# Filling the pair table with blank rows during the second layer instead of the first

## The reference, cut to what matters

```python
# x, ctx: 64 tiles of 128 tokens, 256 features, f32
x = x + ssm(layernorm(x))                    # layer 0: convolution, state space mix, gate
x = x + rope_attention(layernorm(x), ctx)    # 16 heads
x = x + recurrence(layernorm(x))             # scanned over the 64 tiles
x = x + gqa_attention(layernorm(x))          # layer 1: 16 heads on 4 kv heads
x = x + cross_attention(layernorm(x), ctx)   # one head of 256
# mixture of experts
scores = sigmoid(xf @ gate_w.T + lb_bias)
topw, topi = top_k(scores, 2)                # 8 experts, two for each token
for e in range(8):
    sel = (topi == e).any(-1)
    wmean = (topw * (topi == e)).sum() / max((topi == e).sum(), 1)
    out = out + where(sel, mlp_e(xf) * wmean, 0)
x = x + out + shared_mlp(xf)
```

## Time and profile before

| | us |
|---|---|
| median of 3 runs | 3413.04 |
| lowest and highest | 3412.17, 3423.11 |
| the profiled execution, its own time | 3413.31 |
| its span | 3411.5 |
| granted clock over the span | 0.969 of full speed |

### The profile page before, as it was taken

One profiled execution on the slowest core, in us unless ns is written; L12 is line 12 of the kernel. 1 busy time (PEld: TensorE's weight loads), 2 busy tenths in 40 slices (PEclk: granted clock), 3 DMA queues, 4 the chain that ended last, 5 costly groups with the idle time before them and its releaser, 6 DMA issues. The chain is left out here.

```text
span 3411.5 us, 95859 instructions
## 1 busy us (share of the span) xinstructions
PE 3081.2 (90%) x27055; PEld 2659.9 (78%) x27056; DVE 2776.1 (81%) x8725; ACT 2258.2 (66%) x8248; POOL 1512.2 (44%) x5113
## 2 busy tenths in 40 slices
PE   6589999999999999999998698999999999499998
PEld 4478888888888888888887577777777777387998
DVE  5588888888888888888885588888888887687776
ACT  3377777777777777777775477777777777143333
POOL 1244444545444444445452155555555554133333
PEclk8699999999999999999999799999999999699999
DMA  6111111111111111111110200000000000023443
GB/s 187 34 39 49 47 41 41 41 47 48 41 41 41 43 51 43 41 41 41 47 48 14 61 20 15 18 15 18 16 18 18 15 19 13 4 105 119 132 136 89
DMA packets 123391, 161.87 MB, mean 47 GB/s; under 512 B 27331, under 2 KB 94832, under 8 KB 123312
## 3 DMA queue, kind: packets, MB, share of 16 engines
q1 hardware_dynamic: 111056, 126.37, 12.7%
q0 software_dynamic: 12256, 34.53, 2.9%
HBM read 102.85 MB, written 61.53 MB: 48 GB/s over the span
## 5 line engine op out<-in xcount | busy, mean ns | idle before, releaser
L385 POOL TENSOR_TENSOR tiny<-tiny 128x1 f32<-128x1 f32 x3456 | 773.3, 224 | 800.0 <-DVE tiny L372 559.2
L802 ACT ACTIVATE work<-bank,att 128x128 f32<-128x128 f32 x2048 | 720.1, 377 | 55.9 <-DVE att L792 50.1
L802 ACT ACTIVATION_READ_ACCUMULATOR work<-bank,att 128x1 f32 x2048 | 444.5, 217 | 0.0
L792 DVE TENSOR_REDUCE att<-bank 128x4 f32<-128x512 f32 x512 | 333.8, 683 | 44.8 <-PE bank L785 44.8
L821 PE MATMUL bank<-const,work 128*128 128x128 f32 x2048 | 317.9, 278 | 30.6 <-ACT work L802 25.8
L785 PEld LDWEIGHTS bank<-work 32*128 32x128 f32 x4096 | 253.2, 189 | 105.7 <-issue 73.9
L1281 DVE SCALAR_TENSOR_TENSOR work<-work,small 128x127 f32<-128x127 f32 (+2 forms) x1152 | 317.7, 345 | 16.5 <-ACT work L1121 11.1
L785 PE MATMUL bank<-work 32*128 32x128 f32 x4096 | 301.9, 286 | 20.6 <-ACT work L1166 2.5
L821 PEld LDWEIGHTS bank<-const,work 128*128 128x128 f32 x2048 | 239.3, 142 | 73.5 <-ACT work L802 56.7
L385 POOL TENSOR_TENSOR tiny<-tiny,const 128x1 f32<-128x1 f32 x1152 | 251.6, 218 | 90.2
L185 PE MATMUL bank<-w1r,workr 128*128 (+2 forms) x802 | 267.8, 334 | 0.4 <-issue 0.2
(11 more groups left out here) (357 smaller groups left out, 8467.5 us busy)
## 6 DMA issues: line engine op xcount, KB each, us to landing
work<-decay_sums SPq DMA_DIRECT2D x64, 512.0 KB, 3.6
work<-pair_rows SPq DMA_DIRECT2D x91, 258.0 KB, 2.7
pair_rows<-extra SPq DMA_DIRECT2D x128, 182.0 KB
work<-in_ctx SPq DMA_DIRECT2D x128, 128.0 KB, 2.1
x_res<-in_x POOLq DMA_DIRECT2D x8, 1024.0 KB, 16.8
recurrence_out<-r_xo_ SPq DMA_DIRECT2D x64, 128.0 KB, 1.7
work<-recurrence_out SPq DMA_DIRECT2D x64, 128.0 KB
out_dram<-work POOLq DMA_INDIRECT x91, 2.8
```

The lines of the kernel that those rows point to most:

```text
L385: e.tensor_tensor(out_, a_, b_, ALU.add if b_ is three_halves else ALU.mult)\
L792: e.tensor_reduce(a_nm[:, 4 * g:4 * g + 4], sc_banks[g % 2][:, :].rearrange("p (h k) -> p h k", k=P), AX.X, ALU.max, negate=True).then_inc ...
L802: last = e.activation(Pb[g % 2][:, c * P:c * P + P], sc_banks[g % 2][:, c * P:c * P + P], ACT.Exp, bias=a_nm[:, 4 * g + c:4 * g + c + 1], ...
```

## The change

`blank_rows` and all that belongs to it moves from `layer0` to `layer1`. The 64 pieces, three DMAs each, keep their size. In layer 1 SP issues piece i-2 at the end of step i, behind `load_context(i-2)`. The sources are no longer buffers of their own: `blank` is `bo_row`, and `blank_end` is four columns of `tiny`. POOL can clear `bo_row` only when it has been read, so it waits for `b_vrow` first, and SP waits for `blank_ready` ahead of step 0 of layer 1, that is ahead of the first `load_output` and of all loads of the experts' weights. At the end of layer 1 SP waits until all blank rows have landed.

```diff
@@ layer0, sync
-                    b = i
-                    if live(b):
-                        blank_rows(b)
-
-                e.wait_ge(S["blank_ready"], 2)
+
                 pipeline(e, 4, step)
                 e.wait_ge(S["r_store"], 16 * NB)
-                e.wait_ge(S["blank"], 3 * 16 * NB)
@@ layer0, gpsimd
-                e.memset(blank_end, 0.0)
-                e.memset(blank, 0.0).then_inc(S["blank_ready"], 1)
-                e.wait_ge(S["blank_ready"], 1)
-                e.iota(blank_end[:, 2:3].bitcast(I32), [[0, 1]], base=TOKENS, channel_multiplier=1)\
-                    .then_inc(S["blank_ready"], 1)
@@ layer1
+        blank, blank_end = bo_row, tiny[:, 64:68]
@@ layer1, sync
+                def blank_rows(b):
...
+                    for at, n_, of in ((0, D, blank), (D, D, blank), (2 * D, 4, blank_end)):
+                        e.dma_start(rows_b[:, :, at:at + n_], of[0:n // 2].unsqueeze(1).to_broadcast([n // 2, 2, n_]))\
+                            .then_inc(S["blank"], 16)
@@ in step(i)
                     b = i - 2
                     if live(b):
                         load_context(b)
+                    b = i - 2
+                    if live(b):
+                        blank_rows(b)
...
+                e.wait_ge(S["blank_ready"], 2)
                 pipeline(e, 2, step, 0, expert_weights)
+                e.wait_ge(S["blank"], 3 * 16 * NB)
@@ layer1, gpsimd
+                e.memset(blank_end, 0.0)
+                e.wait_ge(S["b_vrow"], 1)
+                e.memset(blank, 0.0).then_inc(S["blank_ready"], 1)
+                e.wait_ge(S["blank_ready"], 1)
+                e.iota(blank_end[:, 2:3].bitcast(I32), [[0, 1]], base=TOKENS, channel_multiplier=1)\
+                    .then_inc(S["blank_ready"], 1)
```

More of the change, by code:

```diff
@@ L105 @@
         c_rec c_rinv c_rtr c_rT c_o c_ohi c_olo c_proj c_x2 r_stats r_aggr r_seed r_rs r_xn r_tr r_xnT r_fi
-        r_tfi r_go r_tg r_xo r_store r_a r_b r_d blank_ready blank
+        r_tfi r_go r_tg r_xo r_store r_a r_b r_d
     """.split(),
@@ L116 @@
         d_nmax d_exp d_ptr d_pt d_pv d_rinv d_x5 g_stats g_aggr g_seed g_rs g_xn g_tr g_xnT g_lg
-        g_sum
+        g_sum blank_ready blank
     """.split(),
@@ L749, in decoder @@
         slots = nc.dram_tensor("pair_rows", (SLOTS * P, ROW), F32, kind="Internal").ap()
-        blank, blank_end = wk(D), wk(4)
         def head_cols(blk, odd, g):
@@ L889, in store_output @@
                     e.dma_start(tile(xo_dram, b), r_xo_[:, :]).then_inc(S["r_store"], 16)
[L891 to L898, removed]
                 def step(i):
@@ L1591, in _ @@
                 e.dma_start(dbv_row, d_bv.partition_broadcast(P)).then_inc(S["l1_bias"], 16)
+                def blank_rows(b):
+                    n = SLOTS * P // NB
+                    rows_b = slots[0:NB * n].rearrange("(b p s) d -> b p s d", b=NB, p=n // 2)
+                    rows_b = rows_b[b] if isinstance(b, int) else rows_b[ds(b, 1)].rearrange("o p s d -> p (o s) d")
+                    for at, n_, of in ((0, D, blank), (D, D, blank), (2 * D, 4, blank_end)):
+                        e.dma_start(rows_b[:, :, at:at + n_], of[0:n // 2].unsqueeze(1).to_broadcast([n // 2, 2, n_]))\
+                            .then_inc(S["blank"], 16)
                 def load_output(b):
```

## The result

The changed kernel takes 3458.4 us (median; 3451.2 to 3473.5) where the kernel before takes 3415.6 in the same comparison: a ratio of 1.0129, 95% interval 1.0112 to 1.0146. It is slower by 43 us. Its profiled execution took 3454.8 us, with a span of 3453.0 against 3411.5, so the two traces differ by 41.4 us.

| part of the program | forecast | measured |
|---|---|---|
| up to SP's first issue of layer 1 (mostly layer 0's loop) | -12 | -5.3 |
| from there to the first L1880 (L1874 after) | +2.8 | +1.3 |
| from there to that line's last run, in layer 1's last step | +48 | +46.2 |
| the experts' part, behind it | 0 | -0.8 |
| sum | +38.8 | +41.4 |

A forecast was written before the change was run, and what follows sets the result against it. Neither loop was taken as bound by transfer bandwidth; time on SP's queue counted, with a ring through SP setting layer 1's step after the change. 3413.3 - 12 + 2.8 + 48 = 3452 us, range 3404 to 3483.

The forecast's parts named there:

- what bounds layer 1: Layer 1's loop: blank issues delay the recurrence's tile, so L1880 runs 0.8 us late in 60 steps, +48 us.
- ring: Layer 1: L1880 to PE's L1660, context's issue, blank issues, tile's landing, L1880 again; 16.13 us a step against 15.33.
- Layer 0's term: Layer 0's loop: decay sums issued some 2 us sooner, DVE's wait on them goes; -12 us, lower bound 5, upper 58.
- the floor at 0.73 us: Layer 0: PE/ACT and POOL chains hold the step, so of DVE's 0.96 us wait only 0.23 us a step returns.
- The start of layer 1: SP waits for POOL's cleared buffer ahead of the first tile and weight loads: +2.8 us, bounds 2.3 and 3.5.
- A: The forecast itself: the ring through SP sets layer 1's step, 3452 us, between 3425 and 3483; chance 0.70.
- D: Rival, layer 1: L1880 has more slack than read, issues are hidden, the loop costs nothing; 3404 us, chance 0.10.
- B: Rival, faster: the wait for the sums is layer 0's ring, all 58 us come back; 3394 us, chance 0.10.
- C: Rival, layer 1: open blank writes hold the tile's semaphore, landing 3.7 us, loop costs 150 us; 3554 us, chance 0.07.

The follow-up runs named there:

- the second experiment: Kernel before, with its blank writes kept in layer 0 but issued ahead of store_output instead of behind load_context: 3411.9 us, ratio 0.9995.

## Why the prediction was right

The step of **what bounds layer 1** held in each part. The forecast was a ring of 9.64 + 0.17 + 4.22 + 2.1 = 16.13 us; the terms measured 9.64, 0.17, 4.16 and 2.07 in the median, and the step 16.05. The loop's +46.2 us is made of 59 steps by 0.72 = 42.5, 1.7 in the first four steps, and some 2 in steps longer than the median (the loop is 6.6 us above 59 median steps, before it was 4.7). The last is no more than traces with the same median step differ by: the kernels at 15.33 have loops 1.9 to 4.7 us above 59 median steps. What decided the size was to take the context's issue to the next issue from layer 0, whose three instructions are the same, and to ask whether the lateness of L1880 comes back to the context's release. It does, and so it isn't paid once but in every step.

**Layer 0's term was mis-sized.** It was -12, from 54.6 - 57 x 0.73; it measured -5.3 between the two traces and 4.4 in the mean of all, at its own lower bound. The step that failed is taking the floor at 0.73 us, so that 0.23 us a step come back; 0.07 to 0.10 did. The reason was named there as the bound's: POOL's chain ends up to 0.1 us later when DVE runs beside it. It ended 0.09 later in the median, 0.12 in the steps shown. The floor was taken from a step in which DVE still waited, and what becomes the bound was priced at the speed that it had under the old schedule. The wait moved from L1307 to L1343, 54.6 to 49.3 us. Whether PE's and ACT's chain to the taps, which ends beside it, would have allowed more is open: no run made POOL's chain shorter with the rest left alone.

**The start of layer 1 was mis-sized too**, +1.3 where +2.8 stood with a lower bound of 2.3. SP's delay was as said: 3.14 us between the bias row and the first tile, 0.40 before. The step that failed is "PE had waited 2.66 us for the first of them, so there is no cover". A load issued later was used sooner. From issue to use the first tile took 3.67 us before (1885.74 to 1889.41) and 2.21 after, and the load of r_tfi_ that PE waits for 3.40 and 2.18. All traces agree: 3.15 to 3.67 us for the first tile where it goes out 0.4 us behind the bias row's load, 1.99 to 2.21 where SP was held first:

```profile
1883.16 0.34 SPq L1584 DMA_DIRECT2D work<-recurrence_out  x1
...
1884.02 0.43 SPq L1606 DMA_DIRECT2D r_tfi_<-in_L_ffn_expert_up_w  x1
```
```profile
1885.37 0.42 DVE L1874 TENSOR_TENSOR work<-work,rows 128x256 f32<-128x256 f32 x1 [2.81 <-DMA work<-recurrence_out]
```
```profile
1886.20 1.11 PE L1621 MATMUL bank<-const,r_tfi_ 128*128 128x128 f32 x4 [4.11 <-DMA r_tfi_<-in_L_ffn_expert_up_w]
```

Of the 2.74 us by which SP was held, 1.3 to 1.4 reached DVE and PE. Why the earlier loads took longer was not tried; the bias row's transfer, 0.4 us ahead of them before and 3.1 after, is the nearest candidate. With SP's wait moved two steps on, PE's L1621 comes 4.25 us behind the bias row's issue, against 4.74 before and 6.18 in the changed kernel.

**How near 3452 was by luck.** The ring was right in mechanism and size. The total came within 3 us of the profiled execution (3454.8) because layer 0's error of +6.7 was met by -1.5, -1.8 and -0.8 in the other rows of the table; the median of the runs lies 6.4 above the forecast. One bound was badly worked out: A's lower edge, 3425, takes 24 us for layer 0, which no row gives, and leaves out the 2.8 of the start of layer 1. It did not matter, since the range went down to D's 3404.

**The rivals.** B, all 58 us of layer 0 back, falls with the second experiment: the wait goes and 0.07 us a step come back. C, that the blank writes hold the tile's semaphore, falls: L1874 follows the tile's issue after 2.03 to 2.07 us in the median with three blank transfers ahead of it, with bytes or nearly without. In layer 0 the sums' landing did not change when the blank writes ahead of them were taken away; the median was 3.6 us and is 3.6 (issue to landing, the line of the sums in the changed kernel):

```profile
DMA to landing us min/median/max: 3.3/3.6/4.2
```

By the rule of "DMA: Bandwidth & Descriptors" in the Trainium skill, section "Queues, rings and completion order", it should have fallen if blank writes still open had held it. In the step of the earlier trace rows the DMA engines stood still from 1009.84 to 1010.30, between the blank transfers and the sums, so no blank packets were left to hold it, and whether the rule orders anything can't be seen here. D, hidden slack, falls by the new wait, but half of it is true: there is slack, 3.45 us between the two issues, and the change overspent it by 0.7. With two such issues in place of three, 3.08 us, layer 1's loop lost nothing.

## What to carry to other kernels

A store that nobody in the loop waits for still costs its issuing time to whatever stands behind it in the same queue, so look where in the list it stands before asking how many bytes it moves: here the same 192 issues cost 43 us behind the load that a ring releases, and nothing ahead of it, where the queue would have waited anyway. When a load closes a ring (its consumer's work releases the issue ahead of it), add up the ring and compare it with the step; the difference is slack: within it an issue is free (3.08 and 3.15 us of 3.45 cost nothing here), and beyond it every step pays. When a wait is removed, price the next one with the engine that was waiting now running beside it, not as the old trace shows it.

## What the runs showed of the hardware

- SP's time for a blank issue does not follow the size of the pieces: two issues of 182 pieces hold it for 2.02 us, from the first's start to the second's end, with 1 KB and with 16 bytes. It rises with their number in that form (0.31 to 0.36 us for 91, 0.58 for 160, 0.86 to 0.89 for 182), but issues of 256 and of 512 pieces in other forms took 0.47 and 0.39. Splitting one of 182 pieces in two of half the size added 1.1 us a step.
- The same bytes written from 14 partitions in place of 91 raised the DMA share from 0.14 to 0.21, and the next load's issue held SP for 1.61 us in place of 0.35.
- Three small POOL operations of 0.73 us took 0.91 with DVE's L1292 and L862 beside them throughout, and 0.73 where L1307 was beside their last part alone.
- In the changed kernel the blank transfers were over 0.4 us ahead of the tile's, which started 0.98 us after its issue.
- The first tile of layer 1 was used 2.0 to 2.2 us after its issue where SP had been held since the bias row's load, and 3.2 to 3.7 where it went out 0.4 us behind it.
- TensorE's granted clock in layer 1 fell as its waits grew: 0.99, 0.98, 0.95 and 0.93 with 815, 791, 753 and 751 us busy of 900. With four issues behind the context the steps of full clock had a median of 17.13 us, those of less a mean of 17.92.
